# A cross-attention kernel: score matmuls over 64 rows of both halves of the array instead of 128 rows with zeros

## The reference, cut to what matters

```python
Q = (x @ Wq.T + bq)      # (8, 112, 256) -> 16 heads of 16
K = (ctx @ Wk.T + bk)    # (8, 375, 256)
V = (ctx @ Wv.T + bv)
attn = softmax(Q @ K.T / sqrt(16))          # per batch and head, 112 x 375
context = attn @ V
y = context @ W_o.T + b_o + x
out = (y - mean(y)) / sqrt(var(y) + 1e-5) * gamma + beta
```

## Time and profile before

| | |
|---|---|
| median of 3 runs | 156.63 us (154.4 to 158.67) |
| profiled execution | 157.02 us, span 155.2 us |
| busy in the span | TensorE 134.0 us, its weight loads 116.7, VectorE 105.6, ScalarE 80.4, GpSimd 60.7 |
| first unit / batch starts | 32.92 us, then 51.92, 67.81, 82.66, 97.62, 112.58, 123.81, 135.75 |

### The profile page before, as it was taken

One profiled execution on the slowest core, in us unless ns is written; L12 is line 12 of the kernel. 1 busy time (PEld: TensorE's weight loads), 2 busy tenths in 40 slices (PEclk: granted clock), 3 DMA queues, 4 the chain that ended last, 5 costly groups with the idle time before them and its releaser, 6 DMA issues.

```text
span 155.2 us, 3853 instructions
## 1 busy us (share of the span) xinstructions
PE 134.0 (86%) x1466; PEld 116.7 (75%) x1466; DVE 105.6 (68%) x247; ACT 80.4 (52%) x163; POOL 60.7 (39%) x83
## 2 busy tenths in 40 slices
PE   5799989679979999889998998999899996779850
PEld 4599779468768899769988987899787875667620
...
GB/s 128 358 259 216 269 296 227 159 270 239 301 204 2 102 156 0 169 267 235 135 52 151 4 178 4 155 2 183 24 128 34 4 4 30 4 4 30 4 0 59
...
## 3 DMA queue, kind: packets, MB, share of 16 engines
...
...
## 4 chain that ended last, share of the span: by engine, by line
PE 65%; DVE 11%; DMA 10%; ACT 6%; issue 5%; SPq 1%; POOLq 0%; ACTq 0%; DVEq 0%
PE m_bank L793 19%; PE pv_bank L873 12%; PE st_bank L857 11%; PE mx_bank L834 10%; DMA q_stack<-shift 6%; DVE mx L656 6%; PE m_bank L901 4%; DMA c_raw<-ctxT 3%; PE m_bank L884 2%; ACT pw L561 2%; PE st_bank L793 2%; DMA q_stack<-q_first 1%; DVE q_hl L618 1%; PE m_bank L841 1%; ACT o_normT L552 1%
## 5 line engine op out<-in xcount | busy, mean ns | idle before, releaser
L656 DVE TENSOR_REDUCE mx<-mx_bank 112x1 f32<-112x375 f32 x128 | 64.6, 541 | 20.4 <-PE mx_bank L834 19.8
L561 ACT ACTIVATE pw<-st_bank 125x448 f32<-125x448 f32 x90 | 48.5, 548 | 48.5 <-PE st_bank L857 47.7
L834 PE MATMUL mx_bank<-k_stack,q_stack 128*112 128x376 f32 x128 | 41.3, 351 | 2.2 <-DVE mx L656 1.2
L857 PE MATMUL st_bank<-q_stack,k_stack 128*125 128x224 f32 x180 | 37.7, 294 | 1.7 <-DMA q_stack<-shift 1.7
L857 PEld LDWEIGHTS st_bank<-q_stack,k_stack 128*125 128x125 f32 x180 | 30.0, 190 | 5.5 <-issue 3.0
L834 PEld LDWEIGHTS mx_bank<-k_stack,q_stack 128*112 128x112 f32 x128 | 22.0, 181 | 4.5 <-DVE mx L656 2.4
L359 POOL TENSOR_TENSOR c_hl<-c_raw,c_hl 128x752 fp32r<-128x752 f32 x6 | 10.9, 1814 | 27.5 <-DVE c_hl L612 27.5
L873 PE MATMUL pv_bank<-pw,v_sb 125*17 125x112 f32 x720 | 20.4, 260 | 1.1 <-ACT o_raw L535 1.1
L405 POOL TENSOR_SCALAR var_eps<-mv 112x1 f32<-112x1 f32 x7 | 1.6, 223 | 49.2 <-DVE mv L692 49.2
L793 PE MATMUL m_bank<-c_hl,w_hl 128*128 128x376 f32 x84 | 18.7, 365 | 0.9 <-ACT w_hl L449 0.9
L873 PEld LDWEIGHTS pv_bank<-pw,v_sb 125*17 125x17 f32 x720 | 16.3, 97 | 3.9 <-issue 2.2
...
## 6 DMA issues: line engine op xcount, KB each, us to landing
...
```

What stands on the lines that cost most here:

```text
L561: nc.scalar.activation(p_tile[0:KC, n % PR, :, :], st_of(n)[0:KC, 0:4 * Q].rearrange("p (j q) -> p j q", j=4), ACT.Exp, scale=float(DK) ** ...
L656: nc.vector.tensor_reduce(mx[b % 2][:, h % 2, q_pair(h // 2):q_pair(h // 2) + 1], mx_bank[n % MR][0:Q, 0:KV], axis=AX_X, op=ALU.max, negat ...
L834: nc.tensor.matmul(mx_bank[n % MR][0:Q, 0:KVP], q_stack[k][:, side, q_pair(h // 2), b - Q_STACKS[k][0], :], k_stack[b % 3][:, h // 2, :], ...
L857: last = nc.tensor.matmul(st_of(n)[0:KC, k * 2 * Q:(k + 1) * 2 * Q], k_stack[i % 3][:, 2 * g + k, c * KC:(c + 1) * KC], q_stack[qk][:, :, ...
```

## The change

The stacks for batches 1 to 7 lose their second copy and their zeros: `q_stack[k]` has side 0's Q in rows 0 to 63 and side 1's in rows 64 to 127. A maxima matmul reads only the 64 rows of its head (batch 0 still all 128). A unit is now one side (1 - u % 2), one half of the head pairs and one third of the keys: four matmuls of 64 rows and 112 columns, each with its own load of 125 columns of K. The unit's first maxima matmul, of the other side wherever the order allows it, stands behind the first of the four. K, V and Q are projected over 128 rows as before.

The shift of batch 0 is made in halves of eight heads (`negate_half`, `transpose_max_half`, `take_shift_half`, `stack_shift_half`), 14 maxima matmuls come before unit 0 instead of 20, and batch 2's V projection moves behind it. All jobs have new places. Those of the output follow later: the output projection of batch i - 3 stands in batch i for i = 3, 4, 5. The transpose of a normalised output shares a bank with that of the maxima. For K of batch 3 and later ScalarE copies the projection out (`take_k`), VectorE rounds it (`round_k`), GpSimd subtracts (`subtract_k`). The scaling of the layer norm moves from VectorE to GpSimd, the rounding of the context from VectorE to ScalarE. The clearing of `q_stack[1]` is no longer shared with VectorE. `values` takes two groups of four heads at once, with the exponentials of both sides (`unit_of`).

```diff
--- before.py
+++ after.py
+X1, X2, U_K = 1, 7, 3
+V_UNITS = ((11, 11, 11), (10, 11, 11), (9, 10, 11))
+HALF = UNITS // 2
+V_SLOT = (0, 2, 1)
+NORM_WITH = {3: 0, 4: 1, 5: 2, 6: 4, 7: 5}
+U_MT = (11, 9, X2, X2, X2, X2, 6)
+U_NEGATE = (10, 8, 6, 6, 6, 6, 5)
+
+
+EARLY_HEADS = 14
+EARLY_JOBS = {1: ("Q", 1, 0), 3: ("Q", 1, 1), 5: ("V", 1, 0), 7: ("V", 1, 1), 9: ("MT", 0, 0), 10: ("V", 1, 2),
+              11: ("K", 2, 0), 13: ("K", 2, 1)}
+FIRST_JOBS = {1: (("MT", 0, 1), ("V", 2, 0)), 2: (("V", 2, 1),), 3: (("V", 2, 2),), 4: (("Q", 2, 0),), 5: (("Q", 2, 1),)}
+FIRST_K = 6
...
+HEADS = (1, 1, 3, 1, 1, 1, 1, 1, 3, 1, 1, 1)
+FIRST_HEADS = ((2, 1, 2, 2, 2, 2, 2, 2, 2, 1, 1, 1), (2, 2, 2, 2, 2, 1, 2, 1, 2, 2, 2, 2))
...
-        q_stack = [sb(f"q_stack{k}", [PART, 2, NP, b1 - b0, Q], F32R) for k, (b0, b1) in enumerate(Q_STACKS)]
-        x_hl = (q_stack[2][:, :, :, :, :].rearrange("p s a b q -> p (s a b q)")[:, 0:2 * EC * B * Q]
-                .rearrange("p (s e n) -> p s e n", s=2, e=EC))
+        q_stack = [sb("q_stack0", [PART, 2, NP, 1, Q], F32R)] + [sb(f"q_stack{k}", [PART, NP, b1 - b0, Q], F32R)
+                                                                 for k, (b0, b1) in enumerate(Q_STACKS) if k > 0]
+        x_hl_last = sb("x_hl_last", [PART, 2, EC, Q_STACKS[2][1] * Q - Q_STACKS[2][0] * Q], F32R)
+        x_hl_early = (q_stack[2][:, :, :, :].rearrange("p a b q -> p (a b q)")[:, 0:2 * EC * Q_STACKS[2][0] * Q]
+                      .rearrange("p (s e n) -> p s e n", s=2, e=EC))
+        k_full = sb("k_full", [PART, 2, KVP])
...
+        neg_half = [sb(f"neg_half{t}", [Q, 2, 2, HP], F32R) for t in range(2)]
+        shift_half = sb("shift_half", [2 * NP, Q], F32R)
...
+            def subtract_k(b, t):
+
+                pool.wait_ge(k_hi, 2 * b + t + 1)
+                nc.gpsimd.tensor_tensor(k_hl[b % 2][:, 1, t, :], k_full[:, t, :], k_hl[b % 2][:, 0, t, :].bitcast(F32),
+                                        op=ALU.subtract).then_inc(k_lo, 1)
...
+            def take_k(b, t):
+
+                src = wait_full(act, "K", b, t)
+                if b > AHEAD:
+                    act.wait_ge(k_lo, 2 * (b - 1) + t + 1)
+                nc.scalar.activation(k_full[:, t, :], src[:, 0:KVP], ACT.Identity,
+                                     bias=bqk[:, 2 + t:3 + t]).then_inc(k_taken, 1)
...
+            def stack_shift_half(t):
+
+                act.wait_ge(shift_ready, t + 1)
+                rows = (shift[0], shift_half)[t]
+                for side in range(2):
+                    first = 2 * DK * SPREAD // 2 * side + SPREAD - 1
+                    act.dma_start(q_stack[0][first:first + SIDES + 1:SIDES, side, t:NP:2, 0, :].bitcast(F32),
+                                  rows[NP * side:NP * (side + 1), :].bitcast(F32)).then_inc(half_in[t], 16)
+
+            def stack_shift(b):
+
+                k = q_stack_of(b)
+                act.wait_ge(shift_ready, b + 2)
+                act.dma_start(q_stack[k][SPREAD - 1:SPREAD + 3 * SIDES:SIDES, :, b - Q_STACKS[k][0], :].bitcast(F32),
+                              shift[b % 2][:, :].bitcast(F32)).then_inc(shift_in[b % 2], 16)
+
+            stack_shift_half(0)
+            v_part(1, 1)
...
+            def round_k(b, t):
+
+                dve.wait_ge(k_taken, 2 * (b - AHEAD) + t + 1)
+                dve.wait_ge(k_in[(b - 2) % 3][t], 48 * ((b - 2) // 3 + 1))
+                nc.vector.tensor_copy(k_hl[b % 2][:, 0, t, :], k_full[:, t, :]).then_inc(k_hi, 1)
...
+            def negate_half(t):
+
+                dve.wait_ge(max_read, H // 2 * (t + 1))
+                src = mx[0][:, :, t:NP:2]
+                hi = neg_half[t][:, :, 0, :]
+                nc.vector.tensor_tensor(hi, src, src, op=ALU.max).then_inc(neg_hi, 1)
+                dve.wait_ge(neg_hi, t + 1)
+                nc.vector.tensor_tensor(neg_half[t][:, :, 1, :], src, hi.bitcast(F32), op=ALU.subtract).then_inc(neg_ready, 1)
...
-            for n in range(H):
+            for n in range(EARLY_HEADS):
                 head_max(n)
                 if n - 4 in range(2):
                     q_lo_part(1, n - 4)
-            negate(0)
-            take_shift(0)
-            for t in range(2):
-                k_lo_part(2, t)
-            for n in range(H, EARLY_HEADS):
-                head_max(n)
+                if n == H // 2 - 1:
+                    negate_half(0)
+                if n == H // 2 + 1:
+                    take_shift_half(0)
+                if n == 12:
+                    k_lo_part(2, 0)
...
                 k = q_stack_of(b)
-                if h < 2 and b == Q_STACKS[k][0]:
-                    pe.wait_ge(q_in[k][h], 48)
+                if b == 0 and h < 2:
+                    pe.wait_ge(q_in[0][h], 48)
+                if b >= 1 and b == Q_STACKS[k][0] and h == 0:
+                    pe.wait_ge(q_in[k][0], 48)
                 if n >= MR:
                     pe.wait_ge(max_read, n - MR + 1)
                 side = h % 2
-                nc.tensor.matmul(mx_bank[n % MR][0:Q, 0:KVP],
-                                 q_stack[k][:, side, q_pair(h // 2), b - Q_STACKS[k][0], :],
-                                 k_stack[b % 3][:, h // 2, :], start=True, stop=True).then_inc(max_full, 1)
+                rows = slice(64 * side, 64 * side + 64) if b >= 1 else slice(0, PART)
+                q = (q_stack[0][rows, side, q_pair(h // 2), 0, :] if b == 0 else
+                     q_stack[k][rows, q_pair(h // 2), b - Q_STACKS[k][0], :])
+                nc.tensor.matmul(mx_bank[n % MR][0:Q, 0:KVP], q, k_stack[b % 3][rows, h // 2, :],
+                                 start=True, stop=True).then_inc(max_full, 1)
+
...
+            def transpose_max_half(t):
+                dst, full = claim("MT", 0, t)
+                pe.wait_ge(neg_ready, t + 1)
+                nc.tensor.transpose(dst[0:2 * NP, 0:Q], neg_half[t][:, :, :, :].rearrange("q s l a -> q (s l a)").bitcast(F32),
+                                    ident[0:Q, 0:Q]).then_inc(full, 1)
...
             def transpose_max(b):
                 dst, full = claim("MT", b)
-                pe.wait_ge(neg_ready, b + 1)
-                nc.tensor.transpose(dst[0:2 * 2 * NP, 0:Q], neg_m[b % 2][:, :, :, :].rearrange("q l s a -> q (l s a)").bitcast(F32),
+                pe.wait_ge(neg_ready, b + 2)
+                if b in NORM_WITH:
+                    norm_columns(dst, NORM_WITH[b])
+                nc.tensor.transpose(dst[0:2 * 2 * NP, D:D + Q], neg_m[b % 2][:, :, :, :].rearrange("q s l a -> q (s l a)").bitcast(F32),
                                     ident[0:Q, 0:Q]).then_inc(full, 1)
 
-            def shifted_scores(i, u):
-                n, g, c = UNITS * i + u, u // NC, u % NC
+            def shifted_scores(i, u, heads):
+                n, half, c, side = UNITS * i + u, u // HALF, u % HALF // 2, 1 - u % 2
                 qk = q_stack_of(i)
-                if u == 0:
-                    pe.wait_ge(shift_in[i % 2], 16 * (i // 2 + 1))
+                if i == 0 and u % HALF == 0:
+                    pe.wait_ge(half_in[half], 32)
+                if i >= 1 and u == 0:
+                    pe.wait_ge(shift_in[i % 2], 16 * ((i + 1) // 2))
                 if n < WIDE + 2:
                     if n >= 2:
                         pe.wait_ge(exp_done, n - 1)
...
                     pe.wait_ge(max_read, B * H)
                 else:
                     pe.wait_ge(exp_done, n - len(wide_ring) + 1)
-                for k in range(2):
-                    last = nc.tensor.matmul(st_of(n)[0:KC, k * 2 * Q:(k + 1) * 2 * Q],
-                                            k_stack[i % 3][:, 2 * g + k, c * KC:(c + 1) * KC],
-                                            q_stack[qk][:, :, q_pair(2 * g + k), i - Q_STACKS[qk][0], :], start=True, stop=True)
+                rows = slice(64 * side, 64 * side + 64)
+                for p in range(HP):
+                    a = HP * half + p
+                    q = (q_stack[0][rows, side, q_pair(a), 0, :] if i == 0 else
+                         q_stack[qk][rows, q_pair(a), i - Q_STACKS[qk][0], :])
+                    last = nc.tensor.matmul(st_of(n)[0:KC, p * Q:(p + 1) * Q],
+                                            k_stack[i % 3][rows, a, c * KC:(c + 1) * KC], q, start=True, stop=True)
+                    if p == 0:
+                        for h in heads:
+                            scores_for_max(h)
                 last.then_inc(st_full, 1)
...
+            projects = {"K": k_project, "Q": q_project, "V": v_project, "MT": lambda b, t: transpose_max_half(t)}
+            for n in range(EARLY_HEADS):
                 scores_for_max(n)
                 if n in EARLY_JOBS:
                     kind, *at = EARLY_JOBS[n]
+                    if n == 9:
+                        pe.wait_ge(ident_ready, 1)
                     projects[kind](*at)
-            pe.wait_ge(ident_ready, 1)
-            transpose_max(0)
-            v_project(2, 2)
-            for n in range(H, EARLY_HEADS):
```

(70 more changed lines are left out.)

370 lines of the change are left out of this document (196 added, 174 removed).

## The result

The changed kernel takes **188.81 us**, the median of four runs (186.18 to 192.0), against 156.2 for the kernel before beside it (four runs, 154.4 to 158.67). The ratio is 1.199 with an interval of 1.178 to 1.220: slower, by far more than the 162.7 forecast and outside the range of 149 to 170. Some executions of most kernels here take several us longer at a lower granted clock, and the ratios leave these out (of the changed kernel they use 186.18 and 186.93). The profiled execution took 186.93 us (span 185.1), 29.9 more than the profiled one of before.

What follows compares the result with a forecast made beforehand. TensorE was taken as the bound (134.0 of 155.2 us busy). Terms -1.3 + 16.3 - 13.4 + 4.5 = +6.1 on the profiled 157.0 gave 163.1, less 0.4 for the median: 162.7 us, range 149 to 170.

Steps and rivals of the forecast that it cites:

- B: TensorE's array mode changes around 64-row runs: 114 changes, 0.20 us into wide weights, 0.09 into value matmuls; 16.3 us more.
- C: Waits that go, among them the output projection's, the start's and low clock after idle time: 13.4 us less.
- A: TensorE's score stream: 64-row halves run side by side, but weight loads double; 1.3 us less.
- the one with queued loads: Rival: the two row halves load weights one after another; 178 us, chance 0.09.
- the one with the whole array: Rival: hardware treats 64 rows as the whole array, nothing runs side by side or drains; 162 us, chance 0.05.
- The rival with free changes: Row halves change mode for nothing at the 99 changes; 148 us, chance 0.17.
- the one that paid only the emptying: Rival: next weights are loaded ahead across a mode change, so only emptying the array costs; 152 us, chance 0.14.
- The output projection's five waits: In C: waits for the transposed norm, 3.5 us idle in 5 places, about 4.5 us saved by later projections.
- The start: In C: halved first shift brings the first scores at 28.5 instead of 32.92 us, 4.4 sooner; 1.3 stay after moved work.
- D: Waits that come: exponentials, second half transpose, shift of batch one; 4.5 us more.
- the exponential: In D: the third unit in a row waits for the first one's exponential, 0.3 us in 10 places, 3.0.
- the half transpose: In D: VectorE's queue in the first units makes the second half transpose late, TensorE standing behind it; 1.0 us.

Runs made afterwards that it cites:

- the later half transpose: Changed kernel with the transpose of the second half of batch zero's maxima at unit 4 instead of unit 1: 189.75 us, ratio 1.199.
- all rows: Changed kernel, order kept, with every score matmul reading all 128 rows, so the 64-row mode is never entered: 177.6 us, ratio 1.139.
- 112 trips with whole rows: Kernel before with a tiny matmul in a 32-column tile ahead of each maxima matmul of batches 1 to 7: 182.26 us, ratio 1.165.
- whole-row work: Kernel of the later half transpose with 28 unused 128-row matmuls added to projections in units one to seven of batch zero: 187.68 us, ratio 1.182.
- the one-unit move: Kernel before with the transpose of the normalised output after unit 8 instead of 9: 157.64 us, ratio 1.013.
- the halves alone: Kernel before with the first shift in halves, first units after 14 heads, all score matmuls over 128 rows: 161.27 us, ratio 1.034.
- the trial with zeros in the Q stacks: Not named further; seemingly the halves alone: kernel before, halved first shift, Q stacks with zeros as before, 161.27 us.

## Why the prediction was wrong

The direction was right, the size was not: 188.81 for 162.7. The direction is not luck: the mode changes of B, which held, outweigh all else in the sum. In the profiled executions +29.9 for +6.1, so 23.8 are to be accounted for.

**The step that failed** is the last one of C: "TensorE had 3.5 us at clock 0.52 right after idle time; the new start leaves it less idle, so 1.7 go." It took a fall behind idle time as the only kind and its length as given, and forecast −1.7. Measured, by the traces, is +13 to +16, a difference of 15 to 18, two thirds of the error or so. Idle time alone is not what did it: the later half transpose filled it and the clock fell for 23.9 us. What makes the stretch long is shown: the matmuls over 64 rows. The maxima alone over 64 rows turn a fall of 3.4 us in the kernel before into 23.9 (mean clock 0.923 to 0.933 in all four executions), and all rows shorten it to 6.8 in the changed one. Some 10 of the 34 us by which the clock is low for longer stay with all rows and belong to the new order, with its waits.

Three things stay open. Whether it is the idle half of the rows or the mode changes that come with it: 112 trips with whole rows made no fall, but no run has many such trips while the clock is low. What lets it fall: in the seven kernels with whole rows that fell ahead of the tail, TensorE had a wait of 1 us or more that ended at most 2.9 us before each of the 12 falls (not every such wait has a fall behind it), while with 64-row matmuls the kernel of the later half transpose and the one with whole-row work fell, the first time, behind no wait over 0.35. And why it stays up in the steady batches, where the same 64-row units alternate with projections.

The Trainium skill, "TensorE: Matmul & The Clock Gate", section What's actually happening, has the clock follow how busy TensorE has been. By that a TensorE busy for 23.30 of 23.90 us, as the profile counts busy, should have run at full clock; the trace differs, and the measurement decides.

**A** was right in kind: the halves run beside each other, 0.01 apart. Of the rivals, the one with queued loads and the one with the whole array are out. That all rows leave batch three at 18.1 says that side by side gives no more than about what its own mode changes cost.

**B** was right: 0.20 from the 64-row scores into a projection at 107.65, as for column tiles. Over a whole trip between two K projections the starts lie 0.32 further apart than at their pace: 0.08 and 0.05 on the way in, 0.09 and 0.10 on the way out. The forecast's two times 0.20 hold one score's own 0.107, and A has 0.05 of stream beside them, so it comes to 0.34. The rival with free changes, which carried 0.17, and the one that paid only the emptying, 0.14, are out. A 64-row maxima matmul among whole-row ones costs 0.21 net (3.3 in 16), with the 0.6 us idle of the batch before gone and some pairs side by side.

**C**, apart from the clock, was too high. The output projection's five waits stood for 4.5; the one-unit move shows 0.3 a batch, so about 1.5. What it waited for comes late for the next in line. The start came 6.0 sooner for 4.4, but not free: with whole rows the halves alone lose 7.8 in batch zero for 2.8 at the start, where I had a gain of 1.3 in C and a loss of 1.5 in D. In the changed kernel the idle part is small (0.4 for the shift, 1.3 for the second half). How much of its batch zero is this, apart from the clock, stays open: the trial with zeros in the Q stacks had its shift land 5.5 us after the copy at a DMA share of 0.92, the changed kernel's 3.2 us, at 0.78. The zeros that I costed at nothing may be that difference; it was not tried.

**D** had the exponential at 3.0 (2.7 measured) and the half transpose at 1.0 (1.3), and left out the three maxima banks. Two units of a steady batch have three maxima each; side by side they are issued within 0.3 us, where VectorE takes 0.54 for each, and in the second place a normalisation of 0.42 stands ahead of them too. That is 1.8 us a batch against nothing; spreading them gave back 1.6. With it, batches three and four would have been 16.5 for my 16. "TensorE standing behind VectorE's maxima in the first two batches for more than 2 us" was named as a sign of being wrong, and it came: 4.4 us idle there, 3.9 of them behind negations. Two of these, 2.6 us, are the transposes of the maxima, for which D had 0.5. The negations ahead of them took 1.40 and 0.78 us for twice 0.17 while GpSimd subtracted K's parts, so "K's split goes to ScalarE, VectorE and GpSimd in turn, but its K is read one and a half batches later, so nothing" left out that VectorE waits for GpSimd there: some 1.5 us.

The terms: 15 to 18 for the clock, 5.5 more behind the maxima banks (6.7 less 1.2), 2.1 for the two transposes (2.6 less 0.5), some 3 short in C (the five waits), less 1.6 for the start (6.0 less 4.4), are 24 to 27 against 23.8. They are estimates from separate runs; the lower figure for the clock fits them better, and the moved work in batch zero is not in them.
